# Attention score products on their head's 64 rows of the array, without zero-padded copies of q and k

## The reference, cut to what matters

```
Q, K = _rope_pair(x @ Wq + bq, x @ Wk + bk);  V = x @ Wv + bv
scores = jnp.einsum('bhqd,bhkd->bhqk', Q, K)
scores = jnp.where(causal, -jnp.inf, scores)
attn = jax.nn.softmax(scores / jnp.sqrt(jnp.float32(HEAD_DIM)), axis=-1)
ctx = jnp.einsum('bhqk,bhkd->bhqd', attn, V)
```

## Time and profile before

| | |
|---|---|
| median of 3 runs | 1535.83 us (1524.18 to 1539.87) |
| span of the profiled execution | 1503.3 us |
| attention, from the first turn of unit 0 to the last product's turn | 292 to 630 us of it |
| PE busy | 81% of the span |
| DVE busy | 66% |
| ACT busy | 54% |

### The profile page before, as it was taken

How to read it: one execution, slowest core, us unless ns; L and a number is a source line. 1 busy time by engine, 2 the same in 40 slices (tenths; PEclk the granted TensorE clock), 3 DMA queues, 4 the chain that set the end, 5 groups by cost and what they waited for, 6 DMA issues and landing times.

```text
span 1503.3 us, 29165 instructions
## 1 busy us (share of the span) xinstructions
PE 1218.4 (81%) x10602; PEld 809.0 (54%) x10640; DVE 986.3 (66%) x1922; ACT 806.5 (54%) x1581; POOL 707.1 (47%) x586
## 2 busy tenths in 40 slices
PE   3879998589989999787999989945578888884994
PEld 2657676334444444365677747532456666663553
DVE  5897656777777777378766643236578888885222
ACT  4667675326666666676666723224645665541221
POOL 2766556771111110066456545323168887782222
PEclk9999999679999999989999995867578998886897
DMA  6200000000000000011000011110411111101122
GB/s 198 69 29 0 1 1 1 1 0 1 2 1 0 1 1 1 1 56 57 1 1 0 1 41 49 42 36 4 153 48 41 41 34 39 38 15 65 55 59 69
DMA packets 57320, 47.03 MB, mean 31 GB/s; under 512 B 20955, under 2 KB 50403, under 8 KB 56293
## 3 DMA queue, kind: packets, MB, share of 16 engines
q1 hardware_dynamic: 55141, 41.08, 9.2%
q0 software_dynamic: 2048, 4.20, 0.9%
HBM read 31.06 MB, written 14.20 MB: 30 GB/s over the span
## 4 chain that ended last, share of the span: by engine, by line
PE 46%; DVE 20%; issue 14%; ACT 13%; POOL 3%; DMA 2%; SPq 2%; DVEq 0%; POOLq 0%; ACTq 0%
PE ps L716 12%; PE ps L904 4%; PE ps L867 4%; PE ps L1016 4%; DVE maxima L1898 3%; PE ps L887 3%; PE ps L817 2%; DVE xn L1664 2%; ACT hr L1183 2%; PE ps L988 2%; ACT arena L1295 2%; DVE arena L1969 2%; ACT arena L1183 2%; PE ps L801 2%; PE ps L785 2%
## 5 line engine op out<-in xcount | busy, mean ns | idle before, releaser
L1559 POOL TENSOR_TENSOR arena<-arena 128x512 f32<-128x512 f32 x126 | 215.2, 1727 | 84.2 <-ACT arena L1295 35.8
L1898 DVE TENSOR_REDUCE maxima<-ps 128x1 f32<-128x512 f32 (+3 forms) x320 | 190.5, 634 | 59.2 <-PE ps L870 39.7
L716 PE MATMUL ps<-xp,wup 128*128 128x512 f32 x768 | 207.2, 415 | 13.4 <-ACT hr L1183 9.6
L1583 POOL TENSOR_TENSOR hr<-arena,hr 128x512 fp32r<-128x512 f32 x128 | 172.2, 1351 | 86.1 <-ACT hr L1183 86.1
L716 PE MATMUL ps<-hr,wdn 128*128 128x512 f32 x768 | 200.3, 410 | 4.1 <-issue 3.0
L1295 ACT ACTIVATE arena<-ps 128x512 f32<-128x512 f32 x256 | 143.6, 597 | 105.5 <-PE ps L988 100.2
L1183 ACT ACTIVATE arena<-ps 128x512 f32<-128x512 f32 x256 | 163.3, 638 | 61.8 <-PE ps L716 61.5
L1249 ACT ACTIVATE arena<-ps 128x1024 f32<-128x1024 f32 (+1 forms) x192 | 150.6, 813 | 73.0 <-PE ps L887 37.0
L1816 DVE TENSOR_TENSOR hr<-arena,hr 128x512 fp32r<-128x512 f32 x128 | 125.0, 989 | 88.3 <-ACT hr L1183 87.2
L716 PEld LDWEIGHTS ps<-xp,wup 128*128 128x128 f32 x768 | 147.1, 198 | 62.5 <-POOL wup L1570 17.6
L716 PEld LDWEIGHTS ps<-hr,wdn 128*128 128x128 f32 x768 | 146.4, 193 | 36.4 <-issue 5.5
(11 more groups left out here) (244 smaller groups left out, 2169.8 us busy)
## 6 DMA issues: line engine op xcount, KB each, us to landing
arena<-up_dram SPq DMA_DIRECT2D x16, 256.0 KB, 2.9
arena<-dn_dram SPq DMA_DIRECT2D x16, 256.0 KB, 3.2
ys_rows<-arena SPq DMA_DIRECT2D x8, 320.0 KB, 2.6
arena<-up_dram SPq DMA_DIRECT2D x2, 1024.0 KB
arena<-dn_dram SPq DMA_DIRECT2D x2, 1024.0 KB
arena<-xs_rows SPq DMA_DIRECT2D x4, 512.0 KB, 4.7
b_parts<-arena SPq DMA_DIRECT2D x1, 1536.0 KB, 5.1
dt_parts<-arena SPq DMA_DIRECT2D x1, 1536.0 KB, 6.2
```

The source lines that it names most:

```text
L716: mm = e.matmul(out, left(a), right(b), start=(first and n == 0), stop=(last and n == 2))
L1559: e.tensor_tensor(hsf[t % 3][:, cols], decayf[u % 2][:, t4 * W + cols.start:t4 * W + cols.stop], hsf[(t - 1) % 3][:, cols], ALU.mult).then ...
L1583: e.tensor_tensor(hr[:, ex % 2, 1, fc, :], hid[:, ex % 2, fc, :], hr[:, ex % 2, 0, fc, :], ALU.subtract).then_inc(MX["rest_pool"], 1)
L1898: e.tensor_reduce(maxf[:, at_max[0]:at_max[-1] + 1:max(1, at_max[-1] - at_max[0])], ps[:, n % 2, 0:ng * w].rearrange("p (g k) -> p g k", g ...
```

## The change

The score products read `qT` and `kT` directly, 64 rows of each (`rows`), so that a head uses its own half of the array's rows. `qz` and `kz`, their 8 copies in a unit and their zeroing are gone; `qT` gets two buffers and `kT` three. In `st` both heads' products now stand together and the two masks behind them. The semaphores `qz_ready`, `kz_ready` and `pads_clear` are gone; ACT's copy of a turned tile waits for the products that last read the buffer. The rotation's work space moves from `qm` to the new buffers' space, and the wait for the second rotation from a turn's copy to the third exponential of unit 0. The loop over units 1 to 4 is written out.

```diff
-        kz = kzf.bitcast(BF16).rearrange("p (s h t) -> p s h t", s=2, h=HG)
-        qz = qzf[:, 0:T].bitcast(BF16).rearrange("p (h t) -> p h t", h=HG)
-        qT = qzf[:, T:T + S].bitcast(BF16).rearrange("p (a t) -> p a t", t=S)
-
-        kT = [f.bitcast(BF16).rearrange("p (a t) -> p a t", t=S) for f in (qzf[:, T + S:T + 2 * S], table)]
+        qT = [qzf[:, n * S:(n + 1) * S].bitcast(BF16).rearrange("p (a t) -> p a t", t=S) for n in range(2)]
+        kT = [kzf[:, n * S:(n + 1) * S].bitcast(BF16).rearrange("p (a t) -> p a t", t=S) for n in range(3)]
...
-            with go.engine.Fori(0, (NU - 4) // 2) as i:
-                go(order(True, True, True), 2 * i + 1, 1, lambda k: word(i, 1 + k))
-                go(order(True, True, True), 2 * i + 2, 0, lambda k: word(i, 2 + k))
...
+            for u in range(1, NU - 2):
+                unit(order(True, True, True), u)
...
                     if n == 0:
                         e.wait_ge(AT["turned_copied"], NTU * v + NTU)
-                        e.wait_ge(AT["qz_ready"], 2 * v + 2)
...
                     for m, (i, half) in enumerate(group):
                         diag = i // 4 == half
-                        mm = e.matmul(ps[:, n % 2, m * w:(m + 1) * w], qz[:, h, i * P:(i + 1) * P],
-                                      kT[vp][:, h // HP, half * 512:half * 512 + w], start=True, stop=not diag)
+                        rows = slice(h % HP * HR, (h % HP + 1) * HR)
+                        mm = e.matmul(ps[:, n % 2, m * w:(m + 1) * w], qT[vp][rows, h // HP, i * P:(i + 1) * P],
+                                      kT[v % 3][rows, h // HP, half * 512:half * 512 + w], start=True, stop=not diag)
                         if diag:
                             mm = e.matmul(ps[:, n % 2, (m + 1) * w - P:(m + 1) * w], identb[:], hide_q[:],
                                           start=False, stop=True)
...
-                        e.wait_ge(AT["kz_ready"], v + 1)
...
+                    diag = j // 4 == half
                     for h in range(2):
-                        bank = 2 + 2 * pair + h
-                        diag = j // 4 == half
-                        mm = e.matmul(ps[:, bank, 0:w], kz[:, vp, 2 * pair + h, j * P:(j + 1) * P],
-                                      qm[:, vp, pair, half * 512 + q0:half * 512 + 512], start=True, stop=not diag)
-                        if diag:
-                            mm = e.matmul(ps[:, bank, 0:P], identb[:], hide_k[:], start=False, stop=True)
+                        rows = slice(h * HR, (h + 1) * HR)
+                        mm = e.matmul(ps[:, 2 + 2 * pair + h, 0:w], kT[v % 3][rows, pair, j * P:(j + 1) * P],
+                                      qm[rows, vp, pair, half * 512 + q0:half * 512 + 512], start=True, stop=not diag)
+                    for h in range(2 if diag else 0):
+                        mm = e.matmul(ps[:, 2 + 2 * pair + h, 0:P], identb[:], hide_k[:], start=False, stop=True)
...
-                    if n == 0 and not (first and k == 0):
-                        e.wait_ge(AT["qz_ready"], 2 * v)
-                    if n == NRE and first and k == 1:
-                        e.wait_ge(AT["rotated"], 2)
-                    if n == NRE and not first:
-                        e.wait_ge(AT["kz_ready"], v - 1)
+                    if n == 0 and not first:
+                        e.wait_ge(AT["s_done"], NSB * (v - 1))
+                    if n == NRE and v >= 3:
+                        e.wait_ge(AT["st_done"], 2 * NST * (v - 2))
...
+                    if v == 0 and n == 2:
+                        e.wait_ge(AT["rotated"], 2)
...
-                e.memset(kz, 0.0)
-                e.memset(qz, 0.0).then_inc(AT["pads_clear"], 1)
...
-                        for h in range(HP):
-                            rows = slice(h * HR, (h + 1) * HR)
-                            ins = e.tensor_copy(qz[rows, HP * n + h, :], qT[rows, n, :])
-                        ins.then_inc(AT["qz_ready"], 1)
...
-                        rows = slice(n % HP * HR, (n % HP + 1) * HR)
-                        ins = e.tensor_copy(kz[rows, vp, n, :], kT[vp][rows, n // HP, :])
```

More of the change, by code:

```diff
@@ L381, in build @@
             "qkv_done", "qkv_copied", "qkv_taken", "rotated",
-            "masks_ready", "pads_ready", "pads_clear", "parts", "unit_split", "v_placed", "turned", "turned_copied", "returned",
-            "returned_copied", "qz_ready", "kz_ready", "s_done", "max_done", "max_part", "negmax_ready",
+            "masks_ready", "pads_ready", "parts", "unit_split", "v_placed", "turned", "turned_copied", "returned",
+            "returned_copied", "s_done", "max_done", "max_part", "negmax_ready",
             "st_done", "exp_done", "pv_done", "o_copied", "o_turned", "o_summed", "o_normed", "ctxT_turned", "ctxT_ready",
@@ L445, in order @@
                     yield ("oturn", -1, 1)
-                if 4 <= m < 4 + HG and pre:
-                    yield ("kz", 1, m - 4)
                 if m == 5:
@@ L454, in order @@
                         yield from [("returned", 1, n) for n in range(NRE)]
-                    if ahead:
-                        yield from [("qz", 2, pair) for pair in range(HG // HP)]
         EARLY = NTB - NTB // B
@@ L476, in opening @@
             yield from turn_items(0)
-            yield from [("qz", 0, pair) for pair in range(HG // HP)]
-            yield from [("kz", 0, h) for h in range(HG)]
             yield from [("s", 0, n) for n in range(NSB)]
@@ L481, in opening, with word, unit @@
             yield from [("returned", 0, n) for n in range(NRE)]
-            yield from [("qz", 1, pair) for pair in range(HG // HP)]
         closing = [("pv", -1, NST - 1), ("ocopy", -1, 1), ("oturn", -1, 1)]
         def units(go):
[L488 to L492, removed]
-            with go.engine.Fori(0, (NU - 4) // 2) as i:
-                go(order(True, True, True), 2 * i + 1, 1, lambda k: word(i, 1 + k))
-                go(order(True, True, True), 2 * i + 2, 0, lambda k: word(i, 2 + k))
[L496 to L499, removed]
+            def word(u):
+                return u // NG * (ST_ * D) + u % NG * (HG * HD)
+            def unit(items, u, first=False):
+                go(items, u, u % 2, lambda k: word(u + k), first)
+            unit(opening(), 0, True)
+            unit(order(False, True, True), 0)
+            for u in range(1, NU - 2):
+                unit(order(True, True, True), u)
+            unit(order(True, True, False), NU - 2)
+            unit(last(), NU - 1)
+            unit(closing, NU)
         @block.sync
@@ L1227, in unit_scalar @@
                     pair, half = piece(n)
-                    if n == 0 and not (first and k == 0):
-                        e.wait_ge(AT["qz_ready"], 2 * v)
-                    if n == NRE and first and k == 1:
-                        e.wait_ge(AT["rotated"], 2)
-                    if n == NRE and not first:
-                        e.wait_ge(AT["kz_ready"], v - 1)
+                    if n == 0 and not first:
+                        e.wait_ge(AT["s_done"], NSB * (v - 1))
+                    if n == NRE and v >= 3:
+                        e.wait_ge(AT["st_done"], 2 * NST * (v - 2))
                     e.wait_ge(AT["turned"], NTU * v + n + 1)
-                    e.copy((qT if n < NRE else kT[vp])[:, pair, half * 512:half * 512 + 512],
+                    e.copy((qT[vp] if n < NRE else kT[v % 3])[:, pair, half * 512:half * 512 + 512],
                            ps[:, 6 + n % 2 if first else 6, :]).then_inc(AT["turned_copied"], 1)
@@ L1873, in unit_vector @@
                     v, vp = u + k, (par + k) % 2
[L1874 to L1878, removed]
-                        for h in range(HP):
-                            rows = slice(h * HR, (h + 1) * HR)
-                            ins = e.tensor_copy(qz[rows, HP * n + h, :], qT[rows, n, :])
-                        ins.then_inc(AT["qz_ready"], 1)
-                    elif what == "kz":
-                        if n == 0:
-                            e.wait_ge(AT["turned_copied"], NTU * v + NTU)
-                            if not first:
-                                e.wait_ge(AT["exp_done"], 2 * NST * u + 2)
-                        rows = slice(n % HP * HR, (n % HP + 1) * HR)
-                        ins = e.tensor_copy(kz[rows, vp, n, :], kT[vp][rows, n // HP, :])
-                        if n == HG - 1:
-                            ins.then_inc(AT["kz_ready"], 1)
-                    elif what == "s":
+                    if what == "s":
                         h, group, w = s_blocks[n]
```

4 lines of the change are left out of this document (2 added, 2 removed).

## The result

The changed kernel takes **1628.84 us** (median of 4 runs, 1614.60 to 1634.14) against 1533.29 before: ratio 1.063, 95% interval 1.0585 to 1.068. It is slower by 95.5 us, where 12 were forecast and "within 1%" held likeliest. The prediction is wrong, and the time lies outside the range of 1516 to 1575.

What follows compares the result with a forecast made beforehand. Neither PE (28.8 us of issue in 38.2) nor DVE (29.7) was taken to fill a unit; they hand each other PSUM banks. Seven units +14 us and the loop -2 gave +12 on the median 1535.8: 1548 us, range 1516 to 1575.

Steps and rivals of the forecast that it cites:

- the standstill: PE's period less its issue, put at 9.4 us of a unit; to absorb part of the new issue.
- Step 1: In `st`, two heads' products on different rows run side by side: 4.0 us less PE issue a unit.
- The rival that they don't run side by side: `st` pairs run one after another: issue +4.0 us more a unit, 1576 us in all; chance 0.05.
- Step 2: Masks between 64-row products: 24 changes of tile a unit become 127, at 0.095 us each, +9.8 us issue.
- The rival that the 64-row tile is free: 64-row products don't count as a change of tile: period -3.5 us, 1507 us in all; chance 0.12.
- Step 3: PE's issue for a unit goes from 28.8 to 34.6 us, 5.8 more.
- B: Rest of the period, 25.45 us (full-width blocks, turns, `oturn`): forecast -1.0 us, bounds -1.8 and +1.5.
- A: A unit's end and two steps of the next, 12.75 us, mostly masked `s` blocks: forecast +3.0, bounds +1.4 and +4.4.
- the rival "the standstill doesn't shrink": The full 5.8 us of issue come on top of each unit: 1575 us in all; chance 0.13.
- Step 4: DVE loses 8 copies, 3.6 of 29.7 us a unit; 1.5 us counted as gained, at the `kz` copies.
- Step 6: Opening: copies gone, at most -2.6 us, against 64 new changes of tile, 6.1 us; taken as 0, bounds -2.6 and +3.
- The clock: Rival: granted clock in the attention units falls from 1.00 to 0.84, +33 us, 1581 us in all; chance 0.05.

Runs made afterwards that it cites:

- run 4: The changed kernel with each mask cut into two 64-row products on its own head's rows, nothing left out: 1521.62 us, ratio to before 0.993.
- run 1: The changed kernel with 128-row products in both `st` and the `s` blocks, no copies, separation of heads left out: 1519.73 us, ratio to before 0.991.
- run 2: The changed kernel with 64-row products in `st` alone, the `s` blocks reading all 128 rows: 1523.00 us, ratio to before 0.992.
- run 3: The changed kernel with 64-row products in the `s` blocks alone, `st` reading all 128 rows: 1573.86 us, ratio to before 1.026.
- run 5: The changed kernel with score products reading all 128 rows but each mask as two 64-row products: 1572.80 us, ratio to before 1.043.
- run 8: The kernel before with its loop over units 1 to 4 written out and nothing else: 1490.52 us, ratio to before 0.989.
- run 7: The changed kernel with every mask added twice, the second right behind the first in the same tile: 1580.21 us, ratio to before 1.046.
- run 10: The changed kernel with every mask added twice, repeated on one chip with the change itself: 1589.39 us, ratio to before 1.054.
- run 9: The changed kernel with no further edit, repeated on another chip: 1611.16 us, ratio to before 1.067.
- run 6: The changed kernel without its masks in both score products: 1484.43 us, ratio to before 0.985.

## Why the prediction was wrong, point by point

Three terms failed. The largest is one that the sum put at nothing: the granted clock in the units was left at 1.00, where it was 0.72 to 0.95, some 58 of the 93 us. The second is how much of the new issue the standstill and DVE's saved copies would take up: 3.9 us of a unit were forecast, 1.6 measured. The third is the opening, +5.9 us where 0 was put. The points in the prediction's order:

*What bounds the kernel* was read with a wrong sum, and this is the first step that went wrong: "28.8 us of issue in 38.2: PE stands still for 9.4 us". `pv` was counted with one pass of its columns. Its operands are fp32, and it appears as eight rows for four heads: two passes. The row was there: from 422.16 to 422.52 it takes 0.36 us with 128 columns. The change of tile is 0.10 of that and the eight starts one after another some 0.05; the remaining 0.21 is two passes of 0.107 (two cycles a column at 2.4 GHz), where I had counted one. The 512-column `pv` of run 4 (400.48, 1.07 us long) comes out in the same way: two passes of 0.427, the starts, and 0.165 of pipeline. Over the 12 steps 4608 columns of one pass were left out, 4608 x 2 / 2.4 GHz = 3.84 us. So PE issued 32.8 of 38.2 us and stood still for 5.4, not 9.4. Run 1, with those 32.8 us and without the copies, has a period of 37.48.

*Step 1, pairs side by side*: right, in mechanism and size (x2 in 0.28 us). The rival that they don't run side by side is refuted.

*Step 2, changes of tile*: right in mechanism, slightly low in price, 0.10 to 0.11 instead of 0.095 us. The rule of the Trainium skill that was weighed there (TensorEngine Tiling (Array Packing), Key Properties: a change of tiling mode drains the engine, another tile of the same mode doesn't) holds for the 64-row tile: 0.16 us after a mask in the change, no gap in run 4, where both sides are 64-row tiles. The rival that the 64-row tile is free is refuted.

*Step 3*: the issue rose by 6.6 us instead of 5.8 (39.4 - 32.8), from the price of a change.

*The standstill* was to take up 1.0 us in B and 1.4 in A, and the copies 1.5. Period less issue is 5.4 before, 4.7, 4.2, 2.9, 5.5 and 2.9 in runs 1 to 5, and 3.8 in the change at full clock: 1.6 us were taken up, copies included. A came out at +4.5 and B at +0.6, A just above its upper bound of +4.4 and B inside the bounds. A unit at full clock is 5.0 us longer, where +2.0 was said and -0.4 to +5.9 bounded. By its own condition, over +3.0 us for a unit, the rival "the standstill doesn't shrink" holds for this part of the loss, though the standstill did shrink somewhat. Its time of 1575 us stays far below the measured one. Which wait kept the rest of the standstill was not tested.

*Step 4, DVE's copies*: worth 0.4 us of a unit (37.92 to 37.48), not the 1.5 in B. A DVE that is full for 5.59 of 5.80 us of a stretch did not set the period.

*Step 5, the loop*: right by the profile, 37.92 for every unit of run 8. The times can't show 2 us.

*Step 6, the opening*: +5.9 instead of 0, outside its bound of +3. The first `pv` comes at 337.2 us before, at 332.5 in run 1 (no copies, whole rows, clock 0.79), at 337.3 in run 4 (64-row tiles alone, each mask as two products, 0.52) and at 343.1 in the change (0.50). So the copies' going gave up to 4.7 us, more than the 2.6 allowed; the 64-row products with their low clock, and the second half of each mask, took 4.8; and the changes of tile 5.8 more. The clock had no place in the step. *Step 7*: +0.5 us, where -1 to 0 was bounded. *Step 8*: right, ACT waits for no work of POOL's there.

*The clock* is the larger half of the loss. It was a rival with a chance of 0.05, priced at a mean of 0.84 for units of the forecast length; in the change the units had 0.72 to 0.95. The seven periods of run 7 add up to 316.4 us at full clock; less the 25 us of the second masks that is 292. So of the 86.6 us more in the change's periods about 28 are tile changes and what they delay, and about 58 are the clock. Both numbers are worked out, not measured, and the 28 may be a few us low: with the one period seen at full clock, 43.24 us, units 1 to 5 alone would be 24.6 us longer than before. That doubling the masks brings the time down (run 10 beside run 9) shows that the clock's part is real.

What lowers the clock is only partly settled. In the units it isn't the half-used rows alone (runs 2, 4 and 6 keep 1.00), nor the number of changes alone (104 and 112 in runs 3 and 5), nor, as run 6 with its few products shows, simply how much of a unit PE spends on columns. That more products of the same kind at the same places keep it up (run 7) is shown. Among the kernels with single masks only the change has both, 64 rows in both products and changes of tile at every mask, and it alone falls in the units; that the two act together fits every run, but no run varies one of them in steps while the other is held. In the opening, which starts at half clock, either is enough to keep it there: half-used rows without changes (run 6, 0.50), or changes with whole-row products (run 5, 0.58 up to its first `pv`). By the rows the change's clock falls at a unit's end or the begin of the next (from 489.86 to 495.44 us the mean is 0.59, and from there to 508.31 it is 0.50), while PE is never idle for long: 1.6 us in all of a 54 us unit. The Trainium skill (TensorE: Matmul & The Clock Gate, Loop structure matters more than you think) ties the clock to idle waits between bursts of products; by that rule it would have stayed up here, and the rows show it falling without such a wait.

## What to carry to other kernels

Before using part of the array's rows, count how often the stream alternates between tiles: each change cost 0.10 to 0.11 us here, twice a 128-column product, and the masks in another tile's shape cost two and a half times what the pairs gained (10.6 us of issue in a unit, by count and price, against 4.0). Bring the small products of the stream into the same tile, even at the price of more of them (run 4). And check a sum of issue time against the rows for a stretch that is known to be full before calling the rest standstill; in the change, a PE that was busy for 52.4 of 54.0 us had lost its clock, which the busy share hides and only the granted clock shows.

## What the runs showed of the hardware that was not expected

- More work made the kernel faster: with 64 additional 128-column products in a unit the granted clock went from 0.72 or 0.85 to 1.00, and the unit from 54 or 48.6 to 46.4 us (runs 9 and 10).
- With the same instructions, units of the change ran at 0.72, 0.85 or 0.95, within an execution and between two; in runs 1, 2 and 4 the steady units repeated to 0.01 us (37.48, 38.04, 37.35).
- A change of tile costs about the same at half clock, 0.11 us. In the change's opening at a clock of 0.50 a mask takes 0.22 us from start to start (296.17 to 296.39), of which 0.107 are its columns at 1.2 GHz:

```profile
296.17 0.29 PE L862 MATMUL ps<-hide_q,identb 128*128 128x128 bf16 x1
296.39 0.29 PE L859 MATMUL ps<-arena 64*128 64x128 bf16 x1
```

- The opening's clock was 0.50 in the change and 0.52 in run 4, whose `s` blocks use 64 rows, and 0.79 in run 1, where they use 128. It was 0.50 in run 6 too, whose opening has half-used rows and neither masks nor changes of tile among its `s` blocks.
